# Second layer's experts: the next step's gate products issued ahead of the low-rank input of the down projection

## The reference, cut to what matters

```
def _fused_linear(x, W, qa, qb, scale, w):
    out = x @ W.T
    a = jnp.einsum('th,krh->tkr', x, qa)
    b = jnp.einsum('tkr,khr->tkh', a, qb)
    mix = jnp.einsum('tkh,tk->th', b, w)
    return out + scale[None, :] * mix

def expert(muW, gW, gqa, gqb, gs, uW, uqa, uqb, us, dW, dqa, dqb, ds, w):
    xe = x + w @ muW.T
    gate = jax.nn.silu(_fused_linear(xe, gW, gqa, gqb, gs, w))
    up = _fused_linear(xe, uW, uqa, uqb, us, w)
    return _fused_linear(gate * up, dW, dqa, dqb, ds, w)
outs = jax.vmap(expert, ...)(...)
y = jnp.einsum('fth,tf->th', outs, scalar).reshape(b, s, h)
```

## Time and profile before

| | |
|---|---|
| median of 3 runs | 1106.91 us (1106.43 to 1107.95) |
| span of the profiled execution | 1107.4 us; the profile lists no other time of its own for it |
| steps of the experts, first to last TensorE instruction | from about 889 us to about 1098 us of the span |
| TensorE busy | 1003.1 us, 91% |
| VectorE, ScalarE, GpSimd busy | 64%, 55%, 42% |

### The profile page before, as it was taken

One profiled execution on the slowest core, in us unless ns is written; L12 is line 12 of the kernel. 1 busy time (PEld: TensorE's weight loads), 2 busy tenths in 40 slices (PEclk: granted clock), 3 DMA queues, 4 the chain that ended last, 5 costly groups with the idle time before them and its releaser, 6 DMA issues. The chain is left out here.

```text
span 1107.4 us, 18941 instructions
## 1 busy us (share of the span) xinstructions
PE 1003.1 (91%) x6066; PEld 819.1 (74%) x6066; DVE 713.3 (64%) x2102; ACT 606.5 (55%) x1650; POOL 464.9 (42%) x481
## 2 busy tenths in 40 slices
PE   7999999998995699759899999988878889999995
PEld 5899898987883599627678888964445568777884
DVE  5766666663676366546655667645787457888785
ACT  3665666555222355436576776556774555555653
POOL 5777767861377444366111110210137214443322
PEclk9999999999997799979999999988998899999998
DMA  6731111000011699624301101001003011122001
GB/s 206 257 129 67 29 30 29 21 10 1 1 53 54 200 362 337 223 84 137 103 25 62 30 20 39 1 25 50 2 1 116 0 57 58 57 71 86 17 1 38
DMA packets 83496, 85.61 MB, mean 77 GB/s; under 512 B 8545, under 2 KB 75943, under 8 KB 83280
## 3 DMA queue, kind: packets, MB, share of 16 engines
q1 hardware_dynamic: 79056, 75.39, 21.0%
q0 software_dynamic: 3072, 7.34, 2.2%
q10 hardware_dynamic: 1280, 1.77, 0.5%
HBM read 63.36 MB, written 22.02 MB: 77 GB/s over the span
## 5 line engine op out<-in xcount | busy, mean ns | idle before, releaser
L569 POOL TENSOR_TENSOR a_qk<-h,a_by_sin 128x512 f32<-128x512 f32 x64 | 81.7, 1277 | 5.0
L352 DVE CUSTOM_DVE_ANT_0 h<-a_score_ps,mask_bf 128x128 f32<-128x128 f32 (+1 forms) x128 | 40.8, 356 | 61.4 <-PE a_score_ps L345 61.3
L1285 POOL TENSOR_TENSOR a_w_l<-a_w,a_w_h 128x256 fp32r<-128x256 f32 x30 | 22.0, 733 | 112.7 <-ACT a_w_h L1478 112.5
L358 ACT ACTIVATE y_moe<-y_moe,a_nmax 128x128 f32<-128x128 f32 x64 | 25.6, 400 | 76.1 <-DVE a_nmax L352 76.1
L452 PEld LDWEIGHTS a_proj_ps<-a_w,xT 128*128 128x128 f32 x512 | 62.0, 192 | 3.1 <-issue 1.2
L452 PE MATMUL a_proj_ps<-a_w,xT 128*128 128x128 f32 x512 | 62.5, 276 | 0.4 <-DVE hT L510 0.4
L1024 POOL TENSOR_TENSOR e_w_l<-e_w,e_w_h 128x512 fp32r<-128x512 f32 x32 | 40.8, 1276 | 52.3 <-ACT e_w_h L1092 52.3
L80 PE MATMUL a_proj_ps<-a_x_l,a_w_h 128*128 128x512 f32 x128 | 57.4, 448 | 1.7 <-POOL a_w_l L574 1.7
L748 PE MATMUL t_y_ps<-wo,attnT 128*128 128x256 f32 x256 | 57.6, 381 | 0.0
L2628 POOL TENSOR_TENSOR m_up_l<-m_up_w,m_up_h 128x1024 fp32r<-128x1024 f32 x8 | 19.5, 2434 | 89.4 <-ACT m_up_h L2600 89.4
L352 DVE CUSTOM_DVE_ANT_0 y_moe<-a_score_ps,mask_bf 128x128 f32<-128x128 f32 (+1 forms) x128 | 40.5, 354 | 18.4 <-PE a_score_ps L345 17.0
(11 more groups left out here) (459 smaller groups left out, 3539.7 us busy)
## 6 DMA issues: line engine op xcount, KB each, us to landing
slots<-zeros SPq DMA_DIRECT2D x4, 2048.0 KB, 7.3
e_rows<-slots SPq DMA_DIRECT2D x32, 256.0 KB, 4.5
e_w<-in_L_ffn_w_dram SPq DMA_DIRECT2D x32, 256.0 KB, 4.7
out_slots<-e_out SPq DMA_DIRECT2D x32, 256.0 KB, 4.2
e_w<-in_L_ffn_w_dram SPq DMA_DIRECT2D x32, 128.0 KB, 4.2
a_w<-in_L_attn_w_q_dram SPq DMA_DIRECT2D x32, 128.0 KB, 2.2
m_up_w<-in_up_dram SPq DMA_DIRECT2D x8, 512.0 KB, 3.8
a_w<-in_L_attn_Wq_dram SPq DMA_DIRECT2D x16, 128.0 KB, 2.2
```

The costliest lines, as they stand in the source:

```text
L352: done = dve.tensor_tensor_reduce(self.probs[:, b, cells], self.score_ps[:, r, cells], self.k.mask_bf[:, cells], -1.0, 3e38, ALU.add, ALU. ...
L358: act.activation(self.probs[:, b, 0:P], self.probs[:, b, 0:P], ACT.Exp, bias=self.nmax[:, b, 0:1], scale=-1.0, accum_out=self.total[:, b, ...
L569: pool.tensor_tensor(qk[:, par, 0 if what == "q" else 1, half * HALF:(half + 1) * HALF], by_cos[:, r, :], by_sin[:, r2, :], ALU.add).then_ ...
```

## The change

In steps 0 to 14 the six matmuls of `gate_up(n + 1, 0)` are issued ahead of `down_input(n)` instead of behind it, with a wait of their own for the silu that reads the bank they overwrite. Nothing else is moved; no instruction that computes is added or removed.

```
                     if n + 1 < N:
                         factors(n + 1)
+                        pe.wait_ge(silu_done, 2 * n + 1)
+                        gate_up(n + 1, 0)
                     down_input(n)
                     if n + 1 < N:
-                        gate_up(n + 1, 0)
                         if n + 2 < N:
                             low_inputs(n + 2)
                         gate_up(n + 1, 1)
```

## The result

| | before | after |
|---|---|---|
| median on record | 1106.67 us (1104.38 to 1107.95, 4 runs) | 1121.07 us (1114.93 to 1123.18, 4 runs) |
| ratio | | 1.0123, 95% interval 1.0096 to 1.0150 |
| the changed kernel again, 8 runs beside 25 of before | 1106.51 us | 1117.34 us, ratio 1.0089 (1.0056 to 1.0122) |
| span of the profiled execution | 1107.4 us | 1121.1 us (that execution took 1122.95 us) |
| first low-rank product of step 0 to the start of the last `down_out` | 193.90 us | 203.15 us |

A forecast was written before the change was run, and what follows sets the result against it. The prediction took TensorE's standing still in the expert steps as the bound. 14 turns of 1.05 us less 5.6 us of removed waits gave +9.1 us on 1106.91 us: 1116.0 us, range 1112 to 1121 us.

The forecast's parts named there:

- The bound: Expert steps: TensorE, 91% busy, bounds them; its standing still counts, 5.9 us in all to be won.
- What is removed: Waits ahead of `down_input`: 0.70 us in each of six odd steps and 1.37 us in step 0, together 5.6 us.
- The six waits for L2907: Ahead of `down_input`'s second half in odd steps 3 to 13: 0.70 us lost each, 4.2 us, all to go.
- What is added: Between `down_input` and `low_inputs`, steps 0 to 13: TensorE stands 1.05 us for VectorE's L2918, 14 times, 14.7 us.
- The return from VectorE: Part of the wait ahead of `low_inputs`: from VectorE's end to TensorE's start, put at 0.06 us.
- The new wait for silu: Ahead of the moved `gate_up(n + 1, 0)`: already satisfied, cost between nothing and 0.09 us a step, taken as nothing.
- The later chain: Behind even-step `down_input`, moved back 1.36 us: later operands still in time, 0.38 us spare at `factors(8)`, 0.5 us at `down_input(7)`.
- The sum: Over the expert steps: 14 x 1.05 - 5.6 = +9.1 us, 1.41 us per pair of steps; chance 0.80.
- not late: Rival at L2918 in odd steps: VectorE late behind `weigh`, up to 4.7 us more, 1120.7 us; chance 0.09.
- The cover did not stay: Rival ahead of `low_inputs`: the turn stays covered and only the gain is left, 1101.3 us; chance 0.03.
- The swing between levels: Rival on TensorE's clock: it falls behind each turn, 19.6 us on 14 turns, 1135.6 us; chance 0.05.
- That nothing happens: Rival: no measurable effect, the turn costing some 0.4 us or moved matmuls waiting for silu, 1107 us; chance 0.03.

The follow-up runs named there:

- cover_odd: Kernel before, with odd steps and step 0 given the change plus `gate_up(n + 1, 1)` between `down_input` and `low_inputs`: 1100.43 us, ratio 0.9946 to before.
- after_again: The changed kernel run once more, unchanged: median 1117.34 us, ratio 1.0089 to before; 203.26 us in the experts' stretch.
- long_turn: The changed kernel with L2919's VectorE work done twice in steps 0 to 13: 211.67 us in the experts' stretch, median 1120.93 us.

## Why the prediction was right, and what was off

- **The bound.** TensorE's standing still decides: shown. Its busy time in a pair is 24.92 us before and 24.90 us after, and cover_odd, with no wait in its steps, is the shortest.
- **What is removed.** The six waits for L2907 are gone. In step 0 the wait for the first operand is too short to be listed: `down_input` starts 0.41 us behind the last moved matmul (908.59 to 909.00), a slot and the 0.18 us that the forecast left there. Step 0, from its first low-rank product to that of step 1, went from 10.98 to 10.65 us, -0.33 us; the forecast was 1.05 - 1.37 = -0.32 us.
- **What is added.** 14 turns of 1.05 us were forecast; 1.07 and 1.09 us were read. The return from VectorE, put at 0.06 us, is 0.11 us in even steps (990.88 to 990.99). The new wait for silu cost nothing: in step 6 the first moved matmul starts one slot behind the last of `factors` (987.05 to 987.27). Its bound of 0.09 us should have read 0.11 us by the prediction's own terms. Step 14, which has no turn, took 11.48 us before and after.
- **The later chain.** GpSimd's low part of the next weights was to be 0.38 us early for `factors(8)`. The rows of after for its making and its use:

```profile
996.32 2.41 POOL L2628 TENSOR_TENSOR m_up_l<-m_up_w,m_up_h 128x1024 fp32r<-128x1024 f32 x1 [13.01 <-ACT m_up_h L2600]
```

```profile
999.16 0.40 PE L80 MATMUL m_a_ps<-m_xe_l,m_up_h 128*128 128x512 f32 x1
```

It ended at 998.73 and was wanted at 999.16, 0.43 us early. The second operand of `down_input(7)`, forecast 0.5 us early, was there at 1001.99 and wanted at 1002.59.
- **The sum.** +9.1 us forecast, +9.25 us in the experts; per pair 1.41 us forecast, 1.42 us measured (26.52 - 25.10). That they agree so closely is in part luck: two terms were a little small and cancel. By the lengths of steps an even step went from 12.17 to 13.28 us, +1.11 us where the forecast had 1.05. An odd step of before took 0.78 us more than step 1, which had no wait (12.94 against 12.16 us); the prediction read 0.70 us around `down_input` alone.
- **The rivals.** VectorE was free at 1003.37 and started L2919 at 1003.47, 0.42 us behind the last matmul (1003.05): not late. The cover did not stay. The granted clock stayed at 1.00 through the pairs, with pauses of 0.8 us twice in 26.5 us. The swing between levels of which the Trainium skill warns (TensorE: Matmul & The Clock Gate, "A second HAM failure mode: psum-queue depth-cycling") did not occur in these steps. That nothing happens fell with the interval.
- **The time.** 1116.0 us was forecast; the 1121.07 us on record are at the very end of the range, 0.07 us past the 1121 us as written. The step that was mis-sized is the one from the experts' sum to a median: I allowed a microsecond for run to run, at the lower end alone, and "what lies around it stays". The runs of before spread from 1101.18 to 1110.66 us, and the start of the experts moved over 9.4 us in two executions of one program. On the second, larger set of runs the median is 1117.34 us.

The record shows what this spread goes with: the mean granted clock of TensorE over an execution. Of the 25 runs of before beside the second set, the one at 0.946 took 1110.64 us and the one at 0.964 took 1101.29 us. Of the changed kernel, the first set has two runs at 0.947, of 1122.95 and 1123.18 us, and each set has one at 0.958, of 1114.93 and 1114.67 us. All that stands ahead of the first `low_inputs`, in the profiles of after, before and after_again (the granted clock is the third number from the end):

```profile
0.00:893.43 893.43, 805.75 (x5010) 660.91 (x5011) 548.48 (x1822) 486.56 (x1421) 389.37 (x408) 0.94 0.26 84
```

```profile
0.00:888.97 888.97, 800.58 (x5011) 657.35 (x5011) 549.35 (x1822) 486.45 (x1421) 389.97 (x408) 0.95 0.26 84
```

```profile
0.00:884.00 884.00, 796.50 (x5011) 653.75 (x5011) 549.05 (x1822) 486.63 (x1421) 389.83 (x408) 0.96 0.26 85
```

The same matmuls take longer where the clock is lower, while in the experts' stretch it is 1.00 in all three. So the first four runs came out 5 us above the forecast by chance, as far as the record shows, and not by a cost of the change. What sets the clock ahead of the experts was not tried.

## What to carry to other kernels

Work that stands between two dependent products of TensorE may be covering a turn through another engine; before it is moved to fill a small wait, price the turn that it leaves open (here 0.7 to 0.8 us were filled in every second step and 1.1 us opened in every one). Fill a wait with one piece of independent work and leave another in front of the next dependence, as cover_odd does, and only in the steps that wait. Where the profile is one execution, compare a stretch that both kernels share rather than the whole span.

## What the runs showed of the hardware

Two VectorE operations of 0.69 us on a 64x512 operand from the matmul's memory, back to back, start 0.61 us apart in long_turn, so a second one adds less than its duration. A turn from TensorE through one such operation and back, with nothing behind it to fill the hole, cost TensorE 1.07 to 1.09 us in after. TensorE kept the full granted clock (1.00) with 14 pauses of 0.8 us, about one in 13.3 us. Ahead of the steps, behind pauses of 1.05 and 2.10 us, its matmuls took 0.63 us in each of the profiles of after and after_again, as in the earlier trace rows; from the first `low_inputs` to step 0 the granted clock was 0.84 and 0.72.
